# A transformer layer on one core: query and key tiles stored as rows of 2 KB, two context buffers

## The reference

```python
x = L0_attn_hidden_states                       # (4, 512, 512)
q = (x @ wq.T + bq).reshape(B, S, 32, 16)       # k and v alike
scores = jnp.einsum('bshd,bstd->bsht', q, k) / np.sqrt(16)
probs = jax.nn.softmax(scores, axis=-1)
context = jnp.einsum('bsht,bstd->bshd', probs, v).reshape(B, S, E)
x = _layernorm(x + context)
dq1, dq2, dq3 = (nf4_quant_dequant(w) for w in (w1, w2, w3))   # blocks of 64, 16 levels
h = jax.nn.silu(x @ dq1.T) * (x @ dq2.T)        # 1376 hidden
x = _layernorm(x + h @ dq3.T)
```

## Time and profile before

| | before |
| --- | --- |
| median of 3 runs | 765.99 us (764.36 to 766.3) |
| the profiled execution, its own time | 765.74 us |
| its span, first to last instruction | 763.9 us |
| PE busy | 682.9 us (89%) |
| DVE busy | 597.1 us (78%) |
| ACT busy | 467.5 us (61%) |
| POOL busy | 108.7 us (14%) |
| DMA packets | 129907, of them under 512 bytes 89360 |

### The profile page before, as it was taken

How to read it: one execution, slowest core, us unless ns; L and a number is a source line. 1 busy time by engine, 2 the same in 40 slices (tenths; PEclk the granted TensorE clock), 3 DMA queues, 4 the chain that set the end, 5 groups by cost and what they waited for, 6 DMA issues and landing times.

```text
span 763.9 us, 14486 instructions
## 1 busy us (share of the span) xinstructions
PE 682.9 (89%) x5818; PEld 557.0 (73%) x5818; DVE 597.1 (78%) x826; ACT 467.5 (61%) x636; POOL 108.7 (14%) x99
## 2 busy tenths in 40 slices
PE   4949999987996978957999999999999999999983
PEld 3838888866875766746888788888887888888761
DVE  2458998969999897986978998998778975544386
ACT  3456879755765747566736788886666774332134
POOL 0003511205020011010011112121110200000022
PEclk9969999998998887977999999999999999999995
DMA  9998999999743536909122452022404101330447
GB/s 210 225 93 134 101 176 147 166 175 160 179 132 96 157 80 194 251 1 344 44 111 84 180 179 82 1 71 72 160 7 161 55 8 28 138 115 13 149 127 165
DMA packets 129907, 95.00 MB, mean 124 GB/s; under 512 B 89360, under 2 KB 110864, under 8 KB 128560
## 3 DMA queue, kind: packets, MB, share of 16 engines
q1 hardware_dynamic: 128704, 91.97, 55.7%
q10 hardware_dynamic: 1136, 2.10, 1.2%
HBM read 59.12 MB, written 34.93 MB: 123 GB/s over the span
## 4 chain that ended last, share of the span: by engine, by line
PE 57%; DVE 22%; issue 7%; DMA 7%; ACT 4%; SPq 1%; POOL 1%; POOLq 0%; DVEq 0%; ACTq 0%
DVE nf_acc L1177 10%; PE ps_p L939 8%; PE ps_s L939 8%; PE ps_s L941 8%; PE ps_p L940 8%; PE ps_s L940 8%; PE ps_p L941 8%; DMA queries_keys<-qk_p 4%; PE ps_s L1022 2%; DVE smax L1210 2%; DVE prob L1214 2%; DMA wst<-in_L_attn_wk 2%; ACT nf_y L784 1%; DVE y_tmp L1233 1%; ACT part L851 1%
## 5 line engine op out<-in xcount | busy, mean ns | idle before, releaser
L1177 DVE SCALAR_TENSOR_TENSOR nf_acc<-nf_y,nf_acc 128x1024 f32<-128x1024 f32 (+4 forms) x266 | 313.7, 1179 | 37.8 <-ACT nf_y L784 26.8
L784 ACT ACTIVATE nf_y<-nf_w,bound_b 128x1024 f32<-128x1024 f32 (+4 forms) x285 | 286.3, 1047 | 9.1 <-DVE nf_acc L1177 8.6
L939 PE MATMUL ps_p<-x_hl,w_hl 128*128 128x512 f32 x192 | 78.4, 408 | 15.5 <-DVE w_hl L1195 11.0
L1324 DVE TENSOR_TENSOR silu<-silu,ps_s 128x512 f32<-128x512 f32 (+1 forms) x44 | 30.1, 685 | 75.4 <-PE ps_s L941 75.3
L704 POOL TENSOR_TENSOR nf_w<-nf_w,nf_rec 128x1024 f32<-128x1024 f32 (+4 forms) x19 | 44.4, 2339 | 310.1 <-DVE nf_rec L1161 310.1
L941 PE MATMUL ps_p<-x_hl,w_hl 128*128 128x512 f32 x192 | 76.2, 397 | 0.0
L940 PE MATMUL ps_p<-x_hl,w_hl 128*128 128x512 f32 x192 | 76.2, 397 | 0.0
L939 PE MATMUL ps_s<-x_hl,f_ha 128*128 128x512 f32 x192 | 75.0, 391 | 1.1 <-DVE f_la L1195 1.1
L941 PE MATMUL ps_s<-x_hl,f_la 128*128 128x512 f32 x192 | 74.9, 390 | 0.0
L940 PE MATMUL ps_s<-x_hl,f_ha 128*128 128x512 f32 x192 | 74.8, 389 | 0.0
L921 ACT ACTIVATE hid_hl<-silu 128x512 fp32r<-128x512 f32 (+1 forms) x44 | 27.8, 632 | 75.8 <-DVE silu L1324 75.8
(11 more groups left out here) (109 smaller groups left out, 1218.6 us busy)
## 6 DMA issues: line engine op xcount, KB each, us to landing
x_hl<-x_parts SPq DMA_DIRECT2D x10, 2048.0 KB, 8.1
queries_keys<-qk_p SPq DMA_DIRECT2D x32, 288.0 KB, 11.2
x_parts<-x_st SPq DMA_DIRECT2D x16, 512.0 KB, 3.9
nf_w<-in_L_ffn_w SPq DMA_DIRECT2D x24, 256.0 KB, 3.2
dequantised<-nf_acc SPq DMA_DIRECT2D x10, 512.0 KB, 3.0
k_st<-queries_keys SPq DMA_DIRECT2D x64, 72.0 KB, 3.6
q_st<-queries_keys SPq DMA_DIRECT2D x8, 576.0 KB, 6.2
v_blocks<-v_t SPq DMA_DIRECT2D x16, 256.0 KB, 4.9
```

Source lines behind the costliest of these rows:

```text
L784: act.activation(nf_y[0:p, at % NY, 0:w], nf_w[0:p, u % 2, 0:w], ACT.Identity, bias=bound_b[0:p, i:i + 1], scale=STEEP).then_inc(s_ny, 1)
L939: pe.matmul(dst, wh, rh, start=start, stop=False)
L1177: dve.scalar_tensor_tensor(out=acc, in0=y, scalar=float(NF4[i + 1]), in1=acc, op0=ALU.min, op1=ALU.max).then_inc(s_nacc, 1)
L1324: dve.tensor_tensor(h, h, ps_s[0:rows, 1], ALU.mult).then_inc(s_hid, 1)
```

## The change

- `queries_keys` becomes `[2, NBK, E, BK]`: a stored tile is 128 rows of 512 numbers, 2 KB each.
- Loads of queries and keys are eight DMAs each for a half-block, each of 16 x 32 pieces of 32 numbers (128 bytes). SP issues the eight of the queries where the one stood, and the keys four and four in the first two groups of `hb + 1`.
- A second context buffer: `ctx[b % 2]`. `LATE` is gone, ACT copies the context of group G in group G + 4, and `back(G)` stands in G + 3 for all.
- The padding columns and their memset on POOL go, and with them `s_pad`.
- Tiles of the feed-forward lie elsewhere in SBUF, since `ctx_1` needs room; the load of the second `x1_hl` now waits for the last product with values (`s_pv`) instead of the last transpose of probabilities.

```diff
-    qk_d = nc.dram_tensor("queries_keys", [2, NHB, Q4, J2, D, H, KS], F32, kind="Internal").ap()
+    qk_d = nc.dram_tensor("queries_keys", [2, NBK, E, BK], F32, kind="Internal").ap()
-    BACK_AT, CONTEXT_AT = {}, {}
-    LATE = {8 * b + 8 + k: 8 * b + 14 + k // 2 for b in range(NBK - 1) for k in range(4)}
-    for G in range(GG):
-        CONTEXT_AT.setdefault(max(G + 4, LATE.get(G, 0)), []).append(G)
-        BACK_AT.setdefault(G + 4 if G % 8 == 2 and G > 8 else G + 3, []).append(G)
+    BACK_AT = {G + 3: [G] for G in range(GG)}
+    CONTEXT_AT = {G + 4: [G] for G in range(GG)}
-        qk_p = sb("qk_p", [P, NQK, 2 * Q4 * J2, KS], F32, proj)
+        qk_p = sb("qk_p", [P, NQK, BK], F32, proj)
-        ctx = sb("ctx", [MV, H, P], F32, att)
+        ctx_0 = sb("ctx_0", [MV, H, P], F32, att)
+        ctx_1 = sb("ctx_1", [MV, H, P], F32, att)
+        ctx = (ctx_0, ctx_1)
-        def load_queries(eng, hb):
-            eng.dma_start(q_st[hb % 2].rearrange("p h n -> p (h n)"),
-                          qk_d[0, hb].rearrange("q j d h n -> (q j d) (h n)")).then_inc(s_ldq[hb % 2], 16)
+        def load_side(eng, i, hb, a):
+            (q, j), (b, e) = divmod(a, J2), divmod(hb, 2)
+            rows, t0 = slice(32 * q + D * j, 32 * q + D * j + D), TB * e + TI * q + TN * j
+            home = q_st[hb % 2][rows, :, 0:TN] if i == 0 else k_st[hb % 2][rows, j, :, 0:TN]
+            eng.dma_start(home, qk_d[i, b].rearrange("(d h) t -> d h t", h=H)[:, :, t0:t0 + TN]
+                          ).then_inc((s_ldq, s_ldk)[i][hb % 2], 16)
-                    sp.wait_ge(s_probT, GG)
+                    sp.wait_ge(s_pv, GG)
-                    sp.dma_start(qk_d[i, 2 * b:2 * b + 2, :, :, Q4 * m:Q4 * m + Q4].rearrange(
-                        "e q j r h n -> (r h) (e q j) n"), qk_p[:, n % NQK]).then_inc(s_stq[n % NQK], 16)
+                    sp.dma_start(qk_d[i, b, P * m:P * m + P], qk_p[:, n % NQK]).then_inc(s_stq[n % NQK], 16)
-                    load_keys(sp, hb + 2, range(0, 2))
-                    load_keys(sp, hb + 1, range(2 + 3 * g, 5 + 3 * g))
+                    load_keys(sp, hb + 1, range(4 * g, 4 * g + 4))
-            pool.memset(qk_p[:, :, :, TN:], 0.0).then_inc(s_pad, 1)
-                if e == 0 and g == 0 and b:
-                    act.wait_ge(s_tr, TURN[("ct", b - 1, len(HEADS) - 1)] + 1)
-                home = ctx[:, :, TI * e:TI * e + TI].rearrange("m h (j n) -> m h j n", j=J2)
+                if e == 0 and g == 0 and b >= 2:
+                    act.wait_ge(s_tr, TURN[("ct", b - 2, len(HEADS) - 1)] + 1)
+                home = ctx[b % 2][:, :, TI * e:TI * e + TI].rearrange("m h (j n) -> m h j n", j=J2)
```

More of the change, by code:

```diff
@@ L293, in layer_kernel @@
         x1_st = sb("x1_st", [P, 2, 2, BK], F32R, att)
+        ctx_1 = sb("ctx_1", [MV, H, P], F32, att)
+        ctx = (ctx_0, ctx_1)
         v_bd = (v_bd_0, v_bd_1)
         att.close()
-        x1_hl1 = sb("x1_hl1", [P, 2, KC, BK], F32R)
+        f3_ha = sb("f3_ha", [P, NJG, E], F32R)
+        hid_hl = sb("hid_hl", [P, 2, 2, BK], F32R)
         f1_ha = sb("f1_ha", [P, 2, KC, NJG * P], F32R)
@@ L301, in layer_kernel @@
         x1_hl0 = sb("x1_hl0", [P, 2, KC, BK], F32R)
-        hid_hl = sb("hid_hl", [P, 2, 2, BK], F32R)
+        x1_hl1 = sb("x1_hl1", [P, 2, KC, BK], F32R)
         silu = sb("silu", [P, 2, BK], F32)
+        f1_lb = sb("f1_lb", [P, 2, KC, NJG * P], F32R)
+        f3_hb = sb("f3_hb", [P, NJG, E], F32R)
         f1_hb = sb("f1_hb", [P, 2, KC, NJG * P], F32R)
-        f1_lb = sb("f1_lb", [P, 2, KC, NJG * P], F32R)
         f3_lb = sb("f3_lb", [P, NJG, E], F32R)
-        f3_hb = sb("f3_hb", [P, NJG, E], F32R)
-        f3_ha = sb("f3_ha", [P, NJG, E], F32R)
+        behind = sb("behind", [P, 1088 // 4], F32)
         f1_la = sb("f1_la", [P, 2, KC, NJG * P], F32R)
@@ L428, in down_over, with load_queries @@
                 eng.wait_ge(s_down, step + 1 - n)
-        def load_queries(eng, hb):
-            eng.dma_start(q_st[hb % 2].rearrange("p h n -> p (h n)"),
-                          qk_d[0, hb].rearrange("q j d h n -> (q j d) (h n)")).then_inc(s_ldq[hb % 2], 16)
+        def load_side(eng, i, hb, a):
[4 more added lines that the diff above has]
+                          ).then_inc((s_ldq, s_ldk)[i][hb % 2], 16)
+        def load_queries(eng, hb, which=range(Q4 * J2)):
+            for a in which:
+                load_side(eng, 0, hb, a)
         def load_keys(eng, hb, which=range(Q4 * J2)):
             for a in which:
-                q, j = divmod(a, J2)
-                eng.dma_start(k_st[hb % 2][32 * q + D * j:32 * q + D * j + D, j].rearrange("d h n -> d (h n)"),
-                              qk_d[1, hb, q, j].rearrange("d h n -> d (h n)")).then_inc(s_ldk[hb % 2], 16)
+                load_side(eng, 1, hb, a)
         def load_w(eng, i, q):
@@ L822, in queries_keys @@
                 wait(act, s_stq[n % NQK], 16 * (n // NQK))
-                act.activation(qk_p[:, n % NQK, :, 0:TN], ps_p[:, tau % 3].rearrange("p (a n) -> p a n", n=TN),
-                               ACT.Identity, bias=bias[:, i, m:m + 1]).then_inc(s_qh, 1)
+                act.activation(qk_p[:, n % NQK], ps_p[:, tau % 3], ACT.Identity, bias=bias[:, i, m:m + 1]
+                               ).then_inc(s_qh, 1)
             def exp(G):
@@ L961, in turn @@
                     for a, h in enumerate(HEADS[c]):
[L962 removed]
+                        t = pe.transpose(dst[:, a * MV:(a + 1) * MV], ctx[k % 2][:, h], ident[0:MV, 0:MV])
                 elif kind == "xt":
@@ L1015, in scores @@
                 if g == 0:
-                    pe.wait_ge(s_ldq[hb % 2], 16 * (hb // 2 + 1))
+                    pe.wait_ge(s_ldq[hb % 2], 16 * Q4 * J2 * (hb // 2 + 1))
                     pe.wait_ge(s_ldk[hb % 2], 16 * Q4 * J2 * (hb // 2 + 1))
```

3 lines of the change are left out of this document (removed).

## The result

| | before | changed |
|---|---|---|
| median of the runs, us | 766.14 (764.36 to 769.76, 4 runs) | 757.78 (757.14 to 760.08, 4 runs) |
| span of the profiled execution, us | 763.9 | 755.7 |
| clock over the span | 0.943 | 0.951 |

The ratio is 0.989, with a 95% interval of 0.985 to 0.993. The change gains 8.4 us where 13 were forecast. The time lies inside the outer range given (746 to 763) and just outside the forecast's own (749 to 757). The sign is certain and the size is 8 to 12 us, depending on the series.

A forecast was written before the change was run, and what follows sets the result against it. PE was taken to bound mid-projection and feed-forward, DVE the attention, with gains in the stalls between and DVE's waits. 765.74 - 2.9 - 4.3 - 5.3 = 753.2, said as 753 us; range 749 to 757, outer 746 to 763.

The forecast's parts named there:

- First stall: PE's 10.98 us wait before projection tile 8: row stores of 1.2 us free ACT's slot sooner, 2.9 us won.
- The input loads are late, and not the stores: Before tile 8: most of the 10.98 us stays, PE still idling 8 us, because input loads are late.
- Last stall: Last three projection tiles: waits for ACT's copies and DVE's v_t go, 0.43 + 2.39 + 1.46 = 4.3 us won.
- Small loads: Query and key loads in 128-byte pieces: 0.73 us each, costing 0 us; tightest before group 8, 1.5 us slack for PE.
- Second buffer: Attention, where each block's normalised rows become x_st: new context order saves DVE waits, 2.0 + 2.0 + 1.3 = 5.3 us.
- The other places in SBUF … cost nothing: Moved tiles in SBUF, with the missing memset and later second x1_hl load: no cost.
- dear loads: Rival: small loads at 0.93 to 1.0 us each hold up projection and half-blocks, 755.1 to 759.3 us; chance 0.12.
- the order gives nothing: Rival: in the attention DVE's idle before x_st only moves to another wait, 758.5 us; chance 0.06.
- The stores give nothing: Rival: in the projection the first store lands no earlier and last-block loads fill the slots, 760.4 us; chance 0.05.

The follow-up runs named there:

- contexts alone: Changed kernel with the old scratch and old loads, so only second context buffer, its order and new SBUF places against the kernel before: 765.35 us, ratio 0.9984.
- rows alone: Kernel before with only rows of 2 KB and small loads; one context buffer, old copy order and old SBUF places: 758.37 us, ratio 0.9896.
- queries early: Changed kernel with SP issuing a half-block's eight query DMAs at its last group's start, ahead of the wait for the dequantised unit: 754.58 us, ratio 0.982.
- 1152 bytes: Changed kernel with the filler ahead of f1_la, f3_la and minus_i 1152 bytes instead of 1088, moving them 64 bytes: 758.24 us, ratio 0.9895.

## Why the prediction was right, and its size wrong

**First stall.** Forecast 2.9 us, measured 4.5 us, and a further 1.2 us between tiles 8 and 45 (109.65 us became 158.15 - 49.68 = 108.5), which the sum did not have: tile 8 itself takes 5.0 us and not 5.6, since its low clock ends sooner (the granted clock from 54 to 60 us was 0.55 before and is 1.00), and the rest lies in the tiles behind. ACT's slot came 3.9 us earlier and not 2.4. Of the 1.5 us between, 0.6 are the row store, which took 0.62 us where the sum had 1.2: the term that was mis-sized. The other 0.9 are the last input load, which lands at 39.65 us and not at 40.6; the sum had taken that as fixed.

Why was the store mis-sized? It was costed by the input loads, 256 rows of 2 KB in 2.35 us, and they still land some 2.4 us apart (33.02, 35.48, 37.91 us), 512 KB each at about 215 GB/s, where the stores behind them go at over 400 (256 KB in 0.62 us). It is not that reading is slower than writing. An input load (line 449) fills 64 of the 128 partitions of `part`, a row store reads all 128. Loads of 128 rows of 2 KB that fill 128 partitions stand in the same trace: two of 256 KB, issued at 457.6 and 458.0 us, land 0.69 us apart. The rate of the DMA engines from 457 to 462 us shows them:

```profile
GB/s 0 0 0 0 0 0 0 0 0 0 0 0 0 213 229 147 147 246 377 442 311 377 246 410 377 410 230 33 0 0 0 0 0 0 0 0 0 0 131 0
```

So a load of the store's own shape would have given the price almost exactly. That the number of partitions is what halves the rate of the input loads fits these rows; no run changed it alone. The bounds named, nothing and 3.7 us, held.

**"The input loads are late, and not the stores."** Right in direction: most of the stall stayed (6.4 of 11 us). The run with later input loads shows it, and shows that more could be had by moving them.

**Last stall.** Forecast 4.3 us; from tile 45 to the first scores 12.84 us (176.68 - 163.84) became 8.25 (166.40 - 158.15), 4.6 us. Right, with its reason: no wait for `qk_p` or `v_t` is left.

**Small loads.** Forecast 0 at 0.73 us a load; the queries of half-block 2 stand 0.74 us apart, all its sixteen loads 0.85, and the place with the least slack was group 8, where about 0.6 us was lost. The price was nearly right and what sets it was not: "The lower end is SP's own pace, 0.49 us" took SP's issue from the value loads. Here it is 0.63 us at the median and 0.73 on average, and SP's pace is nearly all of the price.

**Second buffer.** Forecast 5.3 us in 2.0 + 2.0 + 1.3. In the changed kernel the three boundaries gave 1.6, a loss of 2.9 (2.4 won by group 24, 5.2 lost by group 25), and 1.2: nothing in all. With contexts alone they gave 1.8, 0.2 and 1.3. So the first and the third are near their forecast, and the second is the step that failed. It stands under the small loads: "nothing of DVE's or ACT's stands behind them but the stores of `x_st`, whose first is now behind eight loads of queries, issued some 8 us ahead of it." That is how it goes at the first boundary, where the loads go out from 230.2 us and the first store at 239.9. At the second SP is held at a store of weights until 280.62 us, and the loads' 6.1 us begin there. The row of before that would have told it is SP's own timeline at each boundary, where the same store goes out at 293.02 us and the first `x_st` at 297.24; I read one boundary and multiplied.

**"The other places in SBUF … cost nothing."** They cost 2.5 us, and with `f_la`'s place moved by 192, 448 or 960 bytes its products lose nothing. No row of before could show it.

The account, in us of the trace: forecast 2.9 + 4.3 + 5.3 = 12.5. Measured 4.5 + 1.2 + 4.6 = 10.3 to the first scores, 0.5 more up to group 15 (in spite of the 0.6 lost at group 8), 1.6 at the first boundary, less 2.9 at the second, 1.2 at the third, less 2.5 in the feed-forward: 8.2, which is the difference of the spans. Two effects that were costed at nothing, 5.2 and 2.5 us, outweigh what the stalls gave beyond their forecast (3.1 us). The outer range held because dear loads (755 to 759) were in it, and that was luck: the loads were not dear, the time was lost in another place.

The rival "the order gives nothing" is close to what contexts alone did at the end (0.9984), for other reasons than it gave. "The stores give nothing" is refuted by rows alone, which hold nearly the whole gain.

Open is why the second boundary costs 2.2 us with contexts alone. There SP is not late: the first store of `x_st` goes out at 295.85 us, as soon as DVE is done with it. It lands 5.7 us later, where the first boundary's took 3.1 us (252.50 to 255.57), and ACT waits 2.45 us for it. Ahead of it in the queue stand the store of weights and the queries' long rows, issued at 293.0 and 293.6 us. In the changed kernel with the queries early the landing still takes 4.4 us (283.60 to 288.03). No run took the store of weights away. Open also is which engine's access the 64 and 128 bytes disturb: the means of PE's weight loads read 188 ns at any place (191 for one group with 1152 bytes).

## What to carry to other kernels

When a DMA is split into small ones, cost them at the issuing queue first: here 0.63 us each on SP for 512 pieces, of 128 bytes or of 64, and twice the count made the kernel 56 us slower (one run) while each landed as soon as before. When a transfer is costed by a neighbour, take one that covers as many partitions: loads into 64 ran at half the rate of loads into 128. Where a fixed queue mixes loads with stores that wait for another engine, look at each occurrence and not only the first: the same eight issues cost nothing at one boundary and 5 us at another, and moving them ahead of the wait won 4 us. And when tiles are moved in on-chip memory, compare the mean time of the busiest instruction before and after; six nanoseconds in 390 were 2.5 us.

## What was not expected of the hardware

- fp32 products that read a tile 64 or 128 bytes off a 256-byte grid (counted from another tile of the kernel) take 396 to 397 ns in place of 390 and start 6 to 7 ns further apart (227.4 to 234.5), and products next to them in the same loop take 1 to 3 ns longer (6 in one group at 128 bytes off); at the multiples of 256 bytes nothing is lost. Five distances ran (64, 128, 256, 512 and 0 off 2048), the first in six different kernels.
- Row stores of 128 x 2 KB land 0.62 us apart, where the same 256 KB in 2048 pieces of 144 bytes took 3.7 us: a factor of six for the same numbers stored. Loads of 128 rows of 2 KB into 128 partitions landed 0.69 us apart; input loads of 256 such rows into 64 partitions 2.4 us apart, at about 215 GB/s.
- PE's idle time of 6.4 us ahead of tile 8 is followed by a granted clock of 0.53 (48 to 54 us), one of 2.1 us by 1.00 (46 to 54 us).
